# Projection jobs in another order, and the division by ScalarE, in a two-batch attention stage

## Chip, cores, metric

One core of one Trainium2 chip. The time is the device time of one execution of the whole program, in microseconds, the median of 3 runs.

## What is computed

The program is a chain of layers on an input of 2 x 2048 tokens of width 256. The change touches only the attention of layer 1, here with what surrounds it left out:

```python
qkv = x @ W_qkv                                   # x is the normalised input, 16 heads of 64
q, k, v = (to_heads(t) for t in jnp.split(qkv, 3, axis=-1))
q, k = (t * cos + rotate_half(t) * sin for t in (q, k))
dots = jnp.einsum('bhid,bhjd->bhij', q, k) * scale
dots = jnp.where(causal, neg, dots)
attn = jax.nn.softmax(dots, axis=-1)
out = jnp.einsum('bhij,bhjd->bhid', attn, v)
out = jax.nn.relu(out.reshape(b, n, INNER) @ W_o1) @ W_o2     # and a layer norm
```

The other stages (two blockwise FP4 feed-forwards, a selective scan, two mixtures of experts) are the same in both kernels.

## The kernel before

The heads are processed in pairs, 8 pairs a batch, 16 in all (`STREAM`), one after the other as a pipeline. A turn is the work of one pair t, cut into 40 steps (`STEPS`), 20 for each of its two heads. In step v:

- TensorE computes the scores of piece v (`scores`, up to 1024 columns, keys on the partitions, queries in the columns), weighs piece v-2 with the values (`weigh`), peeks at one slot (`peek`: scores with queries on the partitions, only to find each row's maximum) and does a side job if the table `SIDE` has one for this step;
- ScalarE turns piece v into exponents twice, in fp32 (`prob`) and fp16 (`prob_high`), and then does its share of the side job;
- VectorE subtracts the two of piece v-1 (`low_part`), does `take` if piece v-2 ended a chunk, finds the maximum of the peeked slot (`maximum`, one bank, so the next peek waits for it) and does its share of the side job.

Two banks of scores alternate. The weighed sums `o` of one chunk of 512 queries have one bank; its 65th column is the sum of the exponents. A chunk of queries ends with pieces 1, 5, 11 and 19 of each head, so `take` comes at steps 3, 7, 13, 21, 23, 27, 33 and, one turn later, 1. It reads `o`, divides it into `heads`, and only after its `o_taken` may TensorE open the next chunk.

The peeks run ahead (`LEAD` is 24): at step 16 those of the next pair t+1 begin. They need its queries and keys, in chunks of 512 tokens: query chunk 0 and key chunk 0 at step 16, chunks 1 at step 18, query chunk 2 at step 22, query chunk 3 at step 26, key chunk 2 at step 30 and key chunk 3 at step 32. They are made by the 8 `qk` side jobs of pair t+1, numbered i: even i is query chunk i//2, odd i key chunk i//2. For each, TensorE projects (6 matmuls of 512 columns into the one side bank), ScalarE copies the bank to one of two halves of `raw` (after GpSimd has rotated job i-2), SyncE moves it across partitions by four DMAs (`cross`), GpSimd rotates it in five instructions (`rotate`, lines 1880 to 1887), and SyncE stacks it into `q_both` (four DMAs) or `k_twice` and `k_low` (six). SyncE's order is written out: the crossing of i+1, then the stack of i, and after stack 5 the loads of the next weights. At the end `spread_queries` copies the four query chunks once more, into `q_shift`. Other side jobs of a turn are 4 `v` projections, 4 transposes of `heads` (`turn`), 8 output products (`out`) and 2 rows of maxima (`mrow`). A side job waits until the bank of the one before is read.

The first turn (`BEFORE`) only projects pair 0, with its jobs packed into the first steps, and peeks. The last pair has nothing to project.

## Time and profile before

| what | value |
| --- | --- |
| median of 3 runs | 4981.34 us (4978.41 to 4983.54) |
| the profiled execution | 4961.9 us, its span 4960.3 us |
| TensorE, VectorE busy | 3653.6 us (74%), 3715.6 us (75%) |
| ScalarE, GpSimd busy | 2571.2 us (52%), 2373.9 us (48%) |
| granted TensorE clock, mean | 0.869 of full speed |

The profile is of one execution. PE is TensorE (PEld its weight loads), DVE is VectorE, ACT is ScalarE, POOL is GpSimd and SP is SyncE; a q behind a name is that engine's DMA queue. A row of a group names the source line, the engine, the operation, output <- inputs and a count, then the busy time and the mean of one instruction, then how long the engine stood before them and what released it. In a timeline, what stands in brackets at the end is that idle time. Attention fills the stretch from about 2700 to 4475 us.

### The profile page before, as it was taken

How to read it: one execution, taken by the hardware profiler on the slowest of the kernel's cores; microseconds unless marked ns; L12 is line 12 of the kernel's file. 1: busy time of each engine (PE TensorE's matmuls, PEld its weight loads, DVE VectorE, ACT ScalarE, POOL GpSimd, SP SyncE). 2: the span in 40 equal slices, each digit the busy share in tenths (PEclk: the TensorE clock that was granted, in tenths of full speed). 3: DMA queues.
4: the chain of work that ended last, by engine and by line, in shares of the span. 5: the costliest groups of instructions: out<-in, count | busy, mean ns of one | idle time of the engine just before them, and what ended most of it. 6: DMA issues, size and time to landing. Idle time of an engine off the chain costs nothing. (4 is left out here: it accounts for less than half of the span.)

```text
span 4960.3 us, 84705 instructions
## 1 busy us (share of the span) xinstructions
PE 3653.6 (74%) x28907; PEld 2574.3 (52%) x28907; DVE 3715.6 (75%) x4463; ACT 2571.2 (52%) x4134; POOL 2373.9 (48%) x1532
## 2 busy tenths in 40 slices
PE   2997545555555559966945998999989999985495
PEld 1664224444343436655832665666656666664484
DVE  6993589999999989960056998999989899975101
ACT  1222456666666642221312777777767777774131
POOL 0220268888888852202022676665656676600202
PEclk9999877777777779967967999999999999996697
DMA  2000000011000100023632222222222222202254
GB/s 87 0 0 4 7 22 30 30 30 30 30 30 29 31 33 0 0 71 126 190 113 74 54 58 53 59 55 66 55 63 54 54 57 56 54 14 89 81 186 151
DMA packets 236314, 276.23 MB, mean 56 GB/s; under 512 B 63820, under 2 KB 183557, under 8 KB 234561
## 3 DMA queue, kind: packets, MB, share of 16 engines
q1 hardware_dynamic: 223056, 244.85, 18.1%
q0 software_dynamic: 8704, 24.35, 1.4%
q8 instruction: 192, 3.15, 0.3%
q10 hardware_dynamic: 4224, 2.76, 0.3%
q14 instruction: 138, 1.12, 0.1%
HBM read 152.60 MB, written 36.04 MB: 38 GB/s over the span
## 5 line engine op out<-in xcount | busy, mean ns | idle before, releaser
L2255 DVE TENSOR_TENSOR att_b_prob_low<-att_b_prob,att_b_prob_high 128x1024 f16<-128x1024 f32 (+2 forms) x640 | 794.8, 1242 | 63.9 <-ACT att_b_prob_high L2222 61.1
L2220 ACT ACTIVATE att_b_prob<-att_b_score,att_soft 128x1024 f32<-128x1024 f32 (+2 forms) x640 | 633.4, 990 | 218.4 <-PE att_b_score L2133 141.6
L2282 DVE TENSOR_REDUCE att_b_neg_max<-att_b_peek 128x1 f32<-128x1024 f32 (+2 forms) x749 | 666.9, 903 | 47.1 <-PE att_b_peek L2113 31.2
L1030 PE MATMUL mix_scan_hT<-ident,mix_scan_h 128*128 128x128 f32 x1024 | 248.4, 389 | 535.0 <-DVE mix_scan_h L978 500.2
L2222 ACT ACTIVATE att_b_prob_high<-att_b_score,att_soft 128x1024 f16<-128x1024 f32 (+2 forms) x640 | 630.4, 985 | 11.7 <-PE att_b_o L2161 6.6
L1030 PEld LDWEIGHTS mix_scan_hT<-ident,mix_scan_h 128*128 128x128 f32 x1024 | 171.0, 196 | 649.9 <-DVE mix_scan_h L978 442.7
L2157 PE MATMUL att_b_o<-att_b_vh,att_b_prob_high 128*128 128x65 f16 x4352 | 461.8, 195 | 40.1 <-DVE att_b_prob_low L2255 29.3
L2157 PEld LDWEIGHTS att_b_o<-att_b_vh,att_b_prob_high 128*128 128x128 f16 x4352 | 400.8, 98 | 129.7 <-DVE att_b_prob_low L2255 75.9
L2131 PE MATMUL att_b_score<-att_b_q_both,att_b_k_twice 128*128 128x512 f16 (+3 forms) x1280 | 445.6, 348 | 28.7 <-ACT att_b_prob_high L2222 18.5
L2161 PE MATMUL att_b_o<-att_b_vh,att_b_prob_low 128*128 128x65 f16 x4352 | 460.9, 194 | 0.0
L2159 PE MATMUL att_b_o<-att_b_vl,att_b_prob_high 128*128 128x64 f16 x4352 | 460.3, 193 | 0.0
L2133 PE MATMUL att_b_score<-att_b_q_shift,att_b_k_low 65*128 65x512 f16 (+3 forms) x1280 | 441.3, 349 | 0.0
L1422 DVE TENSOR_TENSOR moe_exp_y<-moe_exp_y_ps,moe_b 128x256 f32<-128x256 f32 x64 | 24.2, 420 | 553.3 <-PE moe_exp_y_ps L1370 553.3
L963 DVE RECIPROCAL mix_scan_inv<-mix_scan_inv 128x512 f32<-128x512 f32 x128 | 426.2, 3329 | 13.1 <-POOL mix_scan_inv L840 13.1
L2159 PEld LDWEIGHTS att_b_o<-att_b_vl,att_b_prob_high 128*128 128x128 f16 x4352 | 398.7, 98 | 33.6 <-issue 0.3
L1041 PE MATMUL mix_scan_yT<-mix_scan_hcT,ident 128*128 128x256 f32 x1024 | 414.0, 549 | 0.1
L197 POOL TENSOR_TENSOR ffn_q<-ffn_y,ffn_scale 128x704 f32<-128x704 f32 (+1 forms) x128 | 127.9, 1016 | 597.2 <-DVE ffn_y L191 597.2
L1880 POOL TENSOR_TENSOR att_b_raw<-att_b_raw,att_b_cos 128x512 f32<-128x512 f32 x120 | 182.1, 1517 | 465.4 <-DMA att_b_crossed<-att_b_raw 465.2
L2161 PEld LDWEIGHTS att_b_o<-att_b_vh,att_b_prob_low 128*128 128x128 f16 x4352 | 398.1, 97 | 0.0
L2110 PE MATMUL att_b_peek<-att_b_k_twice,att_b_q_both 128*128 128x512 f16 (+1 forms) x1248 | 345.6, 353 | 42.0 <-DVE att_b_neg_max L2282 33.1
L859 POOL TENSOR_TENSOR mix_scan_dub<-mix_scan_factor,mix_scan_inv 128x1024 f32<-128x1024 f32 x128 | 301.3, 2354 | 38.6 <-POOL mix_scan_inv L855 38.4
L978 DVE TENSOR_TENSOR_SCAN mix_scan_h<-mix_scan_a,mix_scan_state,mix_scan_dub 128x512 f32<-128x512 f32 x256 | 313.1, 1262 | 1.4 <-POOL mix_scan_dub L859 1.4
...
## 6 DMA issues: line engine op xcount, KB each, us to landing
...
mix_scan_b_row<-mix_b_rows SPq DMA_DIRECT2D x128, 256.0 KB, 3.1
att_b_crossed<-att_b_raw SPq DMA_DIRECT2D x512, 64.0 KB, 2.0
att_b_q_both<-att_b_halves SPq DMA_DIRECT2D x240, 64.0 KB, 2.0
att_b_k_twice<-att_b_halves SPq DMA_DIRECT2D x240, 64.0 KB, 2.0
...
```

Source lines behind the costliest of these rows:

```text
L963: dve.reciprocal(one, one).then_inc(inverse_ready, 1)
L1030: last = pe.transpose(hT_ps[:, j * D + m * P:j * D + (m + 1) * P], hs[:, b * W + m * GRP + t * P:b * W + m * GRP + (t + 1) * P], ident[:, :])
L1041: last = pe.matmul(yT_ps[half][:, j * D:(j + 1) * D], ident[:, :], hcT[:, b * W + t * D:b * W + (t + 1) * D], start=(n == 0 and j == 0), s ...
L2131: pe.matmul(out, k_twice[h][:, keys], q_both[h][:, b * SEQ + queries.start:b * SEQ + queries.stop], start=True, stop=False)
L2133: last = pe.matmul(out, k_low[h][0:HEAD + 1, keys], q_shift[h][0:HEAD + 1, queries], start=False, stop=not diagonal)
L2157: pe.matmul(out, prob_high[:, at], v_cols[:, s, 0:HEAD + 1], start=first, stop=False, skip_group_check=True)
L2159: pe.matmul(out_v, prob_high[:, at], vl[:, s * HEAD:(s + 1) * HEAD], start=False, stop=False, skip_group_check=True)
L2161: last = pe.matmul(out, prob_low[:, at], v_cols[:, s, 0:HEAD + 1], start=False, stop=final, skip_group_check=True)
L2220: act.activation(prob[:, at:at + width], score[m % 2][:, 0:width], ACT.Exp, scale=soft[:, 0:1])
L2222: act.activation(prob_high[:, at:at + width], score[m % 2][:, 0:width], ACT.Exp, scale=soft[:, 0:1])\
L2255: dve.tensor_tensor(prob_low[:, at:at + width], prob[:, at:at + width], prob_high[:, at:at + width], ALU.subtract).then_inc(low_ready, 1)
L2282: last = dve.tensor_reduce(neg_max[:, first + col:first + col + 1], peek_bank(kind, s)[:, base:base + nb * P], AX.X, ALU.max, negate=True)
```

## The change

Two independent parts.

First, the list `QK` now says which chunk job i makes, and the steps of jobs 4 to 7 move: query 2 at step 13 (was 12), query 3 as job 5 at step 17 (was job 6 at 18), key 2 as job 6 at step 20 (was job 5 at 15), key 3 at step 24 (was 21). The first three `v` jobs go one step earlier, to 21, 22 and 23. As two query jobs follow each other, the semaphores that count landed stacks are now four, one per kind and per half of the ring, and `rotate`, `spread_queries` and `peek` wait for these.

Second, `take` on VectorE keeps the reciprocal and multiplies the 4 columns of `inv` by a unit, and a new `take` on ScalarE scales the four 64-column parts of `o` into `heads`. It stands behind the exponents of the step and ahead of its side job.

```diff
+QK = [("q", 0), ("k", 0), ("q", 1), ("k", 1), ("q", 2), ("q", 3), ("k", 2), ("k", 3)]
 SIDE = {0: ("qk", 0, 1), 3: ("qk", 1, 1), 4: ("turn", 3, -1), 5: ("out", 6, -1), 6: ("qk", 2, 1), 7: ("out", 7, -1),
-        9: ("qk", 3, 1), 12: ("qk", 4, 1), 15: ("qk", 5, 1), 16: ("mrow", 1, 0), 18: ("qk", 6, 1), 21: ("qk", 7, 1),
-        22: ("v", 0, 1), 23: ("v", 1, 1), 24: ("v", 2, 1), 25: ("turn", 0, 0), 26: ("out", 0, 0), 27: ("out", 1, 0),
-        28: ("v", 3, 1), 29: ("turn", 1, 0), 30: ("out", 2, 0), 31: ("out", 3, 0), 35: ("turn", 2, 0),
+        9: ("qk", 3, 1), 13: ("qk", 4, 1), 16: ("mrow", 1, 0), 17: ("qk", 5, 1), 20: ("qk", 6, 1),
+        21: ("v", 0, 1), 22: ("v", 1, 1), 23: ("v", 2, 1), 24: ("qk", 7, 1), 25: ("turn", 0, 0), 26: ("out", 0, 0),
+        27: ("out", 1, 0), 28: ("v", 3, 1), 29: ("turn", 1, 0), 30: ("out", 2, 0), 31: ("out", 3, 0), 35: ("turn", 2, 0),
...
+        def same_buffer(i):
+            return [u for u in range(QK_JOBS) if QK[u][0] == QK[i][0] and u % 2 == i % 2]
+        def landed(i):
+            return stacked[QK[i][0] + str(i % 2)]
+        def landed_count(p, i):
+            mine = same_buffer(i)
+            return (p * len(mine) + mine.index(i) + 1) * (Q_STACKS if QK[i][0] == "q" else K_STACKS) * 16
...
             if kind != BEFORE or i >= 2:
-                wait_apart(eng, stacked[r], stacked_count(p, i), (tables, 32))
+                wait_for_stack(eng, p, i - 2)
...
-                sp.wait_ge(stacked[0], there)
+                for i in (QK.index(("q", CH - 2)), QK.index(("q", CH - 1))):
+                    there = landed_count(p, i)
+                    sp.wait_ge(landed(i), there if isinstance(p, int) else sp.to_reg(there))
...
                 for v in range(STEPS):
                     if has_piece(kind, v):
                         exponents(t, v)
+                    if v >= 2 and has_piece(kind, v - 2) or v < 2 and has_piece(kind, -1):
+                        take(t, v - 2)
...
+            def take(t, m):
...
+                if h == 0:
+                    wait_unless_first(act, h_turned, turn_count(p - 1, Q + 1))
+                act.wait_ge(inv_ready, chunk_count(p, h, Q) + 1)
+                for i in range(GT):
+                    at = (Q * GT + i) * PAIR + h * HEAD
+                    last = act.activation(heads[:, at:at + HEAD], o_cols[:, i, 0:HEAD], ACT.Identity, scale=inv[:, i:i + 1])
+                last.then_inc(o_taken, 1)
...
-                dve.reciprocal(inv[:, :].unsqueeze(2), o_cols[:, :, HEAD:HEAD + 1]).then_inc(inv_ready, 1)
-                if h == 0:
-                    wait_unless_first(dve, h_turned, turn_count(p - 1, Q + 1))
-                dve.wait_ge(inv_ready, n_chunk + 1)
-                mine = heads[:, Q * GT * PAIR:(Q + 1) * GT * PAIR].rearrange("p (i d) -> p i d", d=PAIR)
-                dve.scalar_tensor_tensor(out=mine[:, :, h * HEAD:(h + 1) * HEAD], in0=o_cols[:, :, 0:HEAD],
-                                         scalar=unit[:, 2:3], in1=inv[:, :].unsqueeze(2).to_broadcast([P, GT, HEAD]),
-                                         op0=ALU.mult, op1=ALU.mult).then_inc(o_taken, 1)
+                dve.reciprocal(inv[:, :].unsqueeze(2), o_cols[:, :, HEAD:HEAD + 1]).then_inc(inv_found, 1)
+                dve.wait_ge(inv_found, n_chunk + 1)
+                dve.tensor_scalar(inv[:, :], inv[:, :], unit[:, 2:3], None, ALU.mult).then_inc(inv_ready, 1)
```

## Rows read from the trace of the kernel before

**Rows 1.** the page: busy time of the engines over the span.

```profile
PE 3653.6 (74%) x28907; PEld 2574.3 (52%) x28907; DVE 3715.6 (75%) x4463; ACT 2571.2 (52%) x4134; POOL 2373.9 (48%) x1532
```

**Rows 2.** stretches: length, busy us per engine (instructions), granted clock, DMA share, GB/s.

```profile
2704.00:4475.00 1771.00, 1629.25 (x20848) 1097.52 (x20846) 1585.37 (x1896) 1316.37 (x1540) 1079.38 (x670) 0.98 0.24 54
3364.65:3473.03 108.38, 101.55 (x1320) 68.74 (x1317) 100.45 (x121) 82.26 (x96) 72.77 (x45) 1.00 0.30 75
```

**Rows 3.** waits in the turn 3364.65 to 3473.03: total us, times, longest.

```profile
ACT att_b_raw L2198 <- POOL att_b_halves L1887: 10.5, 5, 3.2
```

**Rows 4.** timeline of that turn: start, length, engine, operation [idle before <-releaser].

```profile
3399.45 0.59 ACT L2198 COPY att_b_raw<-att_b_side 128x512 f32<-128x512 f32 x1 [2.36 <-POOL att_b_halves L1887]
...
3402.09 2.15 DVE L2255 TENSOR_TENSOR att_b_prob_low<-att_b_prob,att_b_prob_high 128x1024 f16<-128x1024 f32 x1 [1.65 <-ACT att_b_prob_high L2222]
...
3416.57 0.96 DVE L2282 TENSOR_REDUCE att_b_neg_max<-att_b_peek 128x1 f32<-128x768 f32 x1 [0.64 <-PE att_b_peek L2113]
...
3417.03 0.59 ACT L2198 COPY att_b_raw<-att_b_side 128x512 f32<-128x512 f32 x1 [2.90 <-POOL att_b_halves L1887]
...
3418.61 1.21 DVE L2255 TENSOR_TENSOR att_b_prob_low<-att_b_prob,att_b_prob_high 128x384 f16<-128x384 f32 x1 [1.08 <-ACT att_b_prob_high L2222]
...
3424.56 0.59 ACT L2198 COPY att_b_raw<-att_b_side 128x512 f32<-128x512 f32 x1 [3.25 <-POOL att_b_halves L1887]
...
3427.68 0.69 DVE L2299 TENSOR_TENSOR att_b_vl<-att_b_side,att_b_vh 128x512 f16<-128x512 f32 x1 [1.65 <-ACT att_b_vh L2204]
...
3438.65 1.23 DVE L2282 TENSOR_REDUCE att_b_neg_max<-att_b_peek 128x1 f32<-128x1024 f32 x1 [0.97 <-PE att_b_peek L2110]
```

**Rows 5.** same timeline: first, last rotation; last key stack; peek of step 32.

```profile
3371.59 2.16 POOL L1880 TENSOR_TENSOR att_b_raw<-att_b_raw,att_b_cos 128x512 f32<-128x512 f32 x1 [26.95 <-DMA att_b_crossed<-att_b_raw]
...
3443.03 1.16 POOL L1887 TENSOR_TENSOR att_b_halves<-att_b_raw,att_b_halves 128x512 f16<-128x512 f32 x1
...
3447.30 0.60 SPq L1909 DMA_DIRECT2D att_b_k_low<-att_b_halves  x1
...
3455.19 0.38 PE L2110 MATMUL att_b_peek<-att_b_k_twice,att_b_q_both 128*128 128x512 f16 x1 [0.24 <-DVE att_b_neg_max L2282]
```

**Rows 6.** the page, DMA issues: KB each, us from issue to landing.

```profile
att_b_k_twice<-att_b_halves SPq DMA_DIRECT2D x240, 64.0 KB, 2.0
```

**Rows 7.** VectorE's groups in that turn: count | busy us, mean ns | idle.

```profile
L2273 DVE SCALAR_TENSOR_TENSOR att_b_heads<-att_b_o,att_unit,att_b_inv 128x256 f32<-128x256 f32 x8 | 3.9, 484 | 0.6
...
L2268 DVE RECIPROCAL att_b_inv<-att_b_o 128x4 f32<-128x4 f32 x8 | 1.4, 175 | 0.5 <-PE att_b_o L2161 0.5
```

**Rows 8.** timeline around the take at step 33 of that turn.

```profile
3457.89 0.17 DVE L2268 RECIPROCAL att_b_inv<-att_b_o 128x4 f32<-128x4 f32 x1
...
3458.10 0.48 DVE L2273 SCALAR_TENSOR_TENSOR att_b_heads<-att_b_o,att_unit,att_b_inv 128x256 f32<-128x256 f32 x1
3458.50 0.95 DVE L2282 TENSOR_REDUCE att_b_neg_max<-att_b_peek 128x1 f32<-128x768 f32 x1
3458.59 1.11 ACT L2220 ACTIVATE att_b_prob<-att_b_score,att_soft 128x1024 f32<-128x1024 f32 x1
...
3458.73 0.19 PE L2157 MATMUL att_b_o<-att_b_vh,att_b_prob_high 128*128 128x65 f16 x1 [0.41 <-DVE att_b_heads L2273]
...
3459.50 0.55 PE L2110 MATMUL att_b_peek<-att_b_k_twice,att_b_q_both 128*128 128x512 f16 x2
...
3460.50 1.08 DVE L2282 TENSOR_REDUCE att_b_neg_max<-att_b_peek 128x1 f32<-128x896 f32 x1
```

**Rows 9.** ScalarE's groups: exponents in that turn; the scan, whole run.

```profile
L2222 ACT ACTIVATE att_b_prob_high<-att_b_score,att_soft 128x384 f16<-128x384 f32 x8 | 4.7, 586 | 0.6 <-PE att_b_o L2161 0.2
...
L886 ACT ACTIVATE mix_scan_hcT<-mix_scan_hT,mix_CT 128x256 f32<-128x256 f32 x512 | 211.9, 464 | 170.1 <-PE mix_scan_hT L1030 170.1
```

**Rows 10.** ScalarE's timeline: two scan activations; table load ahead of attention.

```profile
1519.43 0.84 ACT L886 ACTIVATE mix_scan_hcT<-mix_scan_hT,mix_CT 128x256 f32<-128x256 f32 x2 [1.53 <-PE mix_scan_hT L1030]
...
2700.03 1.28 ACT L2220 ACT_TABLE_LOAD   x1 [22.00 <-DVE att_b_max_row L2305]
```

54 lines of the change are left out of this document (30 added, 24 removed).

## The prediction, made before the changed kernel was run

> **What bounds the kernel now.** I read the page's busy shares first. VectorE and TensorE are the busiest engines over the whole program [rows 1], but only the stretch that the change touches, the attention of layer 1, counts here. The table of stretches cuts it into turns, one per pair of heads. Both attention batches fill 1771 us. The turn from 3364.65 to 3473.03 us is typical: 108.4 us, VectorE busy 100.5, TensorE 101.6, ScalarE 82.3, GpSimd 72.8, at TensorE's full granted clock [rows 2]. TensorE's busy time counts the drain of pipelined matmuls, so its true load is lower, but VectorE and TensorE are plainly tied: every step hands work from scores to exponents to the low part to the weighing, and peek and maximum share one bank. So a stall lengthens a turn when it stops these two engines together, and ScalarE matters only where it makes them wait.
>
> The waits of that turn say where that happens. ScalarE stood 10.5 us in 5 waits for GpSimd before it could copy a projected chunk; its ring has two places, and GpSimd must have rotated job i-2 first [rows 3]. The timeline shows what each stall did. At step 12 ScalarE waits 2.36 us; the exponents queued behind it come late, and VectorE then stands 1.65. The jobs at steps 18 and 21 hold ScalarE 2.90 and 3.25, and around them VectorE stands 0.64 and 1.08, then 1.65. At step 26 the peek needs the fourth query chunk, whose stack has just landed: VectorE stands another 0.97 [rows 4]. Of these, 0.64 ends on a peek and is the least surely GpSimd's. The sum of these is 1.65 + 0.64 + 1.08 + 1.65 + 0.97 = 5.99 us a turn. Nothing is wrong with GpSimd's total: it is done with the eight rotations at 3444.19 and idle afterwards; the jobs are simply asked for faster (every 3 steps, 8.1 us) than it rotates. From its first step at 3371.59 it rotates six jobs back to back, until 3424.4, 8.8 us each [rows 4, 5].
>
> **The reordering.** Jobs 0 to 3 keep their steps. Query chunk 2 goes from 12 to 13, query chunk 3 from 18 to 17, key chunk 2 from 15 to 20, key chunk 3 from 21 to 24. Count, bytes and matmuls are unchanged. Against the unchanged pace of rotation: job 4 needs the rotation that ended just before 3399.45; ScalarE reaches the copy of step 12 at 3397.1 and gets there one step (2.0 us of exponents) later, so 2.36 falls to about 0.3. Job 5 at 17 finds its place free. Job 6 at 20 needs the end of rotation 4 (3416.9) and comes two steps later than now, which leaves 0 to 1. Job 7 at 24 comes three steps later, which covers 3.25. Query chunk 3 is now job 5, stacked one whole rotation sooner, so the 0.97 goes. I keep 0.7 back for job 6 and for five neighbouring steps (20 to 24) that now all carry side work on TensorE: 5.3 us a turn. Ends: 6.0, and 2.6, the first 1.65 and the 0.97 alone, whose cause the rows name outright.
>
> What is late next is key chunk 3. Its last stack was issued at 3447.30; with 2.0 us to landing [rows 6], it lands at 3449.3, 84.7 us into the turn. The peek of step 32, which needs it, starts at 3455.19, at 90.5 [rows 5]. With 5.3 gained and about 1 given back by then it would start at 86.2, a margin of 1.5 us. On SyncE, job 5 now issues four stacks and job 6 six; the weight loads keep their place behind stack 5, and the crossing of job 7 still queues behind them, so asking for it three steps later costs that rotation little. The copies of the queries into q_shift wait for two counts instead of one, both long met. The prologue's jobs stay packed in steps 0 to 7, ahead of its first peek at 16: nothing.
>
> **The division, VectorE's side.** A take is a reciprocal (0.17) and a scalar_tensor_tensor of 128x256 (0.48) [rows 7]; by starts, 3457.89 to 3458.50, it occupies 0.61 [rows 8]. Afterwards it is the reciprocal, the same 0.21 until its result may be read, and a tensor_scalar of 128x4. No row has it. Bounds: above, what the instruction that it replaces holds VectorE, 0.40 (3458.10 to 3458.50) [rows 8], a gain of nothing; below, the reciprocal of the same 128x4, 0.17 [rows 7], less the 0.08 by which the next instruction starts ahead of an end: 0.1. The size is the reciprocal's, so I take 0.1. VectorE gives up 0.61 - 0.31 = 0.3 us a take, 8 takes a turn: 2.4 us.
>
> **The division, ScalarE's side.** It gets four activations of 128x64 from PSUM with a scale of one column. The selective scan has the same instruction at 256 columns: 464 ns, and two of them in 0.84, so 0.38 from start to start [rows 9, 10]. The exponents take 1.11 at 1024 columns and 0.59 at 384, 0.82 ns a column [rows 8, 9], so 64 columns take 0.16 less than 256: 0.30, and 0.21 apart: 3 x 0.21 + 0.30 = 0.94 us, of which ScalarE is held 0.84; 6.7 us a turn, and its 82.3 becomes 89. Could Identity between Exp ask for a table load? One costs 1.28 and stands once ahead of attention [rows 10]; two a take would be 20 us a turn. But the scan's Identity (line 886, 512 times) runs between the Tanh and Exp of lines 901 and 905, and its group has no load behind it [rows 9]: none is added.
>
> The price is not ScalarE's busy time but the wait it puts into TensorE. The accumulator o has one bank; the weighing that opens the next chunk waits for the take. Now VectorE frees it 0.7 us after its reciprocal starts. Afterwards the take stands in ScalarE's queue behind both exponents of step v, and behind it stand the side copy of that step and the exponents of v+1. At step 33 the exponents end at 3458.59, the four activations would end near 3459.6, and the weighing that opened at 3458.73 (after 0.41 of waiting for VectorE) opens 0.9 later [rows 8]. That delay is not all lost: the next peek would end about 3461.0 instead of 3460.1, and VectorE, which came to it at 3460.50, is 0.3 sooner by its lighter take and waits: the turn loses 0.5. The eight chunk ends (steps 1, 3, 7, 13, 21, 23, 27, 33) differ by the side job that TensorE does in between: where there is a projection (3, 13, 21, 23: about 1.4 us, by the peek's two matmuls in 0.55) TensorE arrives late anyway and the 0.3 may be gained; where there is none or a short one (1, 7, 27, 33) 0.2 to 0.7 is lost. Ends: -0.3 a take (all hidden, VectorE's gain whole) and +0.9 (step 33 everywhere, nothing caught up). I take +0.2, for the majority of the eight lies nearer the lower end: +1.6 a turn. In the last pair there are no peeks in the second half, ScalarE sets the pace and pays 0.84 whole: 5 x 0.84 = +4 once.
>
> **The sum.** 15 turns have both parts (pairs 1 to 15 projected during pairs 0 to 14): 15 x (-5.3 + 1.6) + 4 = -51.5 us. The profiled execution took 4961.9 us (span 4960.3), so 4910 for it; the median of the timed runs is 4981.3, 19 us above, and the same difference gives 4930.
>
> **A rule that speaks against the change.** The take holds VectorE 0.61 us in one instruction of width and would hold ScalarE 0.84 in four [rows 8 to 10]. The Trainium skill (ScalarE: Activation LUTs, Rules for kernel authors) tells to use VectorE, not ScalarE, for a multiplication. By that rule the second part is a loss, which is the second rival below; by the rows it is a loss per take that only matters where TensorE waits.
>
> **Rivals.**
> Both parts pay: the stalls go whole and the takes hide. 15 x (-6.0 - 2.4) = -126 at most, so 4855 to 4905. For it speaks that VectorE is busy for 93% of the turn (100.5 of 108.4); against it, step 33. Chance 0.14.
> ScalarE's take is the new stall (the side of slower): TensorE waits 0.9 at each of the eight chunk ends, 7 us a turn, while the reordering brings its lower end, 2.6: 15 x (7.2 - 2.6) + 4 = +73, up to 5054. With the reordering at 5.3 it decides from a mean of 0.63 us lost per chunk end, and shows from 0.71. For it speaks step 33; against it, the projections that fill the gap at four of eight. Chance 0.13.
> The two cancel within the measurement: 0.55 to 0.71 lost per chunk end, 15 x (-5.3 + 4.4 to 5.7) + 4, 4971 to 4991. Chance 0.12.
> Key chunk 3 becomes the bound: the reordering doesn't do what it says in full, because the peek of step 32 waits for rotation 7 and gives back some 2.5 us a turn: 15 x (-2.8 + 1.6) + 4, 4967. For it: a margin of only 1.5 us. Chance 0.06.
>
> **How the numbers follow.** Forecast 4930, chance 0.55, own range 4905 (stalls gone whole, takes at +0.1: 15 x (-6.0 + 0.8) + 4 = -74) to 4965 (a quarter of the stalls stays, takes at +0.33: 15 x (-4.0 + 2.6) + 4 = -17). The range 4890 to 4988 takes in the cancelling case and the upper part of the first rival. A change under 0.2% (10 us) can't be told from none here. Faster 0.55 + 0.14 + 0.06 = 0.75; same 0.12; slower 0.13.
>
> **What the profile after would show.** Right: in a like turn, ScalarE's waits for GpSimd fall from 10.5 to under 3 us; VectorE's 1.65 waits at steps 14 and 22 are gone; the take's four activations stand about 0.21 apart; turns of 104 to 105.5 us. TensorE's openings wait for ScalarE's heads at steps 1, 7, 27 and 33. Wrong: turns still of 108 with those waits (second rival); peeks of step 32 that wait for a DMA into k_low (the last); projections still waiting for GpSimd at 13 or 20, if rotations stretch beyond 8.8 us.

## The result, and the profile after

The changed kernel takes 5037.77 us in the median of 4 runs (5033.37 to 5043.74), the kernel before 4982.44 (4978.41 to 4987.61): 1.0115 times as long, 95% interval 1.0102 to 1.0128, so 55 us slower. Measured again beside other kernels it was 5034.61 us against 4976.73, a ratio of 1.0124 (1.0108 to 1.0139). The forecast was 4930.

The profiled execution took 5035.53 us. That of before took 4961.9, but 17 of these 73 us lie ahead of the work that the change touches: the selective scan begins at 691.8 us in the one and at 709.0 in the other, which differs from one execution to the next. So the attention of layer 1 is compared by its own length, from the first exponent to the last. The table of stretches of after has the columns of [rows 2]; its two rows are all 16 turns, and the seventh turn, the one whose counterpart stands in [rows 2]:

```profile
2722.10:4519.90 1797.80, 1598.56 (x20745) 1086.50 (x20744) 1602.51 (x1879) 1417.01 (x2030) 1102.77 (x670) 0.98 0.23 52
3397.70:3510.10 112.40, 101.92 (x1322) 69.24 (x1319) 103.26 (x121) 89.38 (x129) 74.00 (x45) 0.98 0.29 72
```

Cut the same way, before is 1746.40 us long, so 51.4 of the 55 us are here. Of these, 8.2 are the last pair's turn alone (84.2 us before, 92.4 after, to the end of the last exponent). The turn went from 108.38 to 112.40 us. ScalarE's busy time rose from 82.3 to 89.4 in it; VectorE's, which was to fall, rose from 100.5 to 103.3.

The waits of that turn, engine and waiting line, what it waited for, total us, times, longest; first ScalarE's, then TensorE's:

```profile
ACT att_b_prob L2254 <- PE att_b_score L2153: 7.4, 9, 1.9
ACT att_b_prob L2254 <- PE att_b_score L2150: 6.4, 11, 1.7
ACT att_b_heads L2243 <- DVE att_b_inv L2304: 3.9, 5, 1.4
...
PE att_b_o L2174 <- ACT att_b_heads L2243: 7.3, 7, 1.7
PE att_b_peek L2127 <- issue: 2.0, 1, 2.0
```

The wait of [rows 3], 10.5 us for GpSimd's rotations, is not among them any more. In its place TensorE waits 7.3 us for ScalarE's heads, at seven chunk ends, and once 2.0 us at a peek. The timeline around the take at step 27 of the turn shows the first of these, with the columns of [rows 8]. Where [rows 8] had 0.21 us from the reciprocal to the division, and the chunk opened at once afterwards, there is now:

```profile
3476.79 0.17 DVE L2302 RECIPROCAL att_b_inv<-att_b_o 128x4 f32<-128x4 f32 x1
3477.00 1.02 DVE L2304 TENSOR_SCALAR att_b_inv<-att_b_inv,att_unit 128x4 f32<-128x4 f32 x1
...
3475.87 2.12 POOL L1895 TENSOR_TENSOR att_b_raw<-att_b_raw,att_b_crossed 128x512 f32<-128x512 f32 x1
...
3478.05 0.93 ACT L2243 ACTIVATE att_b_heads<-att_b_o,att_b_inv 128x64 f32<-128x64 f32 x4 [0.89 <-DVE att_b_inv L2304]
3478.85 1.13 ACT L2254 ACTIVATE att_b_prob<-att_b_score,att_soft 128x1024 f32<-128x1024 f32 x1
...
3479.12 0.19 PE L2174 MATMUL att_b_o<-att_b_vh,att_b_prob_high 128*128 128x65 f16 x1 [1.68 <-ACT att_b_heads L2243]
```

The multiplication of 512 numbers by the unit takes 1.02 us. ScalarE waits 0.89 for it, then needs 0.93, and the weighing opens 0.14 after that, 2.33 us after the reciprocal began; at step 33 of before it was 0.84 [rows 8]. The second wait, at the peek of step 18, follows the stacks of key chunk 1, of which the sixth was issued 0.2 us before TensorE came to the peek:

```profile
3446.40 0.60 SPq L1921 DMA_DIRECT2D att_b_k_low<-att_b_halves  x1
...
3448.56 0.38 PE L2127 MATMUL att_b_peek<-att_b_k_twice,att_b_q_both 128*128 128x512 f16 x1 [1.96 <-issue]
```

The row names "issue", that is, nothing in the profile ends there; in seven other turns the same wait is put down to the DMA into k_low, 16.6 us in seven waits beside 16.9 in seven for "issue". Before, the waits of peeks for k_low were 2.2 us in the whole attention.

### The profile page after: what moved, and what is told of

It is laid out like the page before. It is cut to its first block and busy times, and to the rows that moved or that the text cites. A ratio compares the mean times of both kernels' runs of the same rounds, so it can differ in the third digit from the quotient of the medians.

```text
span 5033.9 us, 85323 instructions
## 1 busy us (share of the span) xinstructions
PE 3660.3 (73%) x28907; PEld 2587.3 (51%) x28907; DVE 3739.0 (74%) x4463; ACT 2679.5 (53%) x4646; POOL 2396.1 (48%) x1532
## 5 line engine op out<-in xcount | busy, mean ns | idle before, releaser
L2289 DVE TENSOR_TENSOR att_b_prob_low<-att_b_prob,att_b_prob_high 128x1024 f16<-128x1024 f32 (+2 forms) x640 | 790.0, 1234 | 34.7 <-ACT att_b_prob_high L2256 29.8
L2174 PE MATMUL att_b_o<-att_b_vh,att_b_prob_high 128*128 128x65 f16 x4352 | 467.0, 195 | 123.6 <-ACT att_b_heads L2243 118.4
L963 DVE RECIPROCAL mix_scan_inv<-mix_scan_inv 128x512 f32<-128x512 f32 x128 | 426.1, 3329 | 12.5 <-POOL mix_scan_inv L840 12.5
L2127 PE MATMUL att_b_peek<-att_b_k_twice,att_b_q_both 128*128 128x512 f16 (+1 forms) x1248 | 344.5, 352 | 51.1 <-issue 16.9
```

What stands on the lines that cost most here:

```text
L963: dve.reciprocal(one, one).then_inc(inverse_ready, 1)
L2174: pe.matmul(out, prob_high[:, at], v_cols[:, s, 0:HEAD + 1], start=first, stop=False, skip_group_check=True)
L2289: dve.tensor_tensor(prob_low[:, at:at + width], prob[:, at:at + width], prob_high[:, at:at + width], ALU.subtract).then_inc(low_ready, 1)
```

## The experiments

**First set: one part at a time.** The change has two parts, and the first question was which of them loses. order_only has the new order of the chunks, with the division as it was; take_only has the old order, with ScalarE's division; unit_folded has the whole change without VectorE's new multiplication. All are timed beside the kernel before (4991.37 us here).

order_only, against the changed kernel:

```diff
-                    if v >= 2 and has_piece(kind, v - 2) or v < 2 and has_piece(kind, -1):
-                        take(t, v - 2)
...
-                dve.wait_ge(inv_found, n_chunk + 1)
-                dve.tensor_scalar(inv[:, :], inv[:, :], unit[:, 2:3], None, ALU.mult).then_inc(inv_ready, 1)
...
+                dve.wait_ge(inv_ready, n_chunk + 1)
...
+                dve.scalar_tensor_tensor(out=mine[:, :, h * HEAD:(h + 1) * HEAD], in0=o_cols[:, :, 0:HEAD],
+                                         scalar=unit[:, 2:3], in1=inv[:, :].unsqueeze(2).to_broadcast([P, GT, HEAD]),
+                                         op0=ALU.mult, op1=ALU.mult).then_inc(o_taken, 1)
```

> The changed kernel, with VectorE's old take (reciprocal and one scalar_tensor_tensor) put back: the reordering alone. Theory A, the take on ScalarE is the whole loss: the reordering alone is faster than before, 4905 to 4965 us, ScalarE's waits for GpSimd gone, but with a new wait of TensorE at the peek of step 18 for key chunk 1 (2 us a turn in the changed kernel's trace). Theory B, the reordering is the loss (five neighbouring side jobs, chunks that land later): slower than before, above 4990 us.

Measured: 4984.38 us (11 runs), 0.9990 of before (0.9981 to 0.9999), between the ranges of the two theories. The new order gains next to nothing, 5 us of the 80 that the prediction gave it. Its trace shows the gain coming and going. The waits of ScalarE for GpSimd fell from 150.5 us in the whole attention to 25.1. By the distance from one step's exponent to the next (medians of seven steady turns) step 12 went from 4.96 to 2.26 us and step 15 from 5.07 to 2.22. But step 17 went from 2.06 to 3.39, step 18 from 3.66 to 6.16, and step 19 from 1.61 to 3.66. Before, TensorE comes to the peek of step 18 at 48.3 us into the turn; now it is there at 46.0, 2.3 us sooner, and the keys are not. The end of the fourth rotation, the last key stack, the peek, and the maximum behind it:

```profile
3426.12 1.44 POOL L1899 TENSOR_TENSOR att_b_halves<-att_b_raw,att_b_halves 128x512 f16<-128x512 f32 x1
...
3430.68 0.60 SPq L1921 DMA_DIRECT2D att_b_k_low<-att_b_halves  x1
...
3432.81 0.59 PE L2127 MATMUL att_b_peek<-att_b_k_twice,att_b_q_both 128*128 128x512 f16 x1 [3.79 <-issue]
...
3433.65 0.82 DVE L2314 TENSOR_REDUCE att_b_neg_max<-att_b_peek 128x1 f32<-128x640 f32 x1 [4.91 <-PE att_b_peek L2130]
```

In the kernel before, in the turn of [rows 2], the same three stand so:

```profile
3405.67 1.71 POOL L1887 TENSOR_TENSOR att_b_halves<-att_b_raw,att_b_halves 128x512 f16<-128x512 f32 x1
...
3410.88 0.60 SPq L1909 DMA_DIRECT2D att_b_k_low<-att_b_halves  x1
...
3413.20 0.43 PE L2110 MATMUL att_b_peek<-att_b_k_twice,att_b_q_both 128*128 128x512 f16 x2 [0.26 <-DVE att_b_neg_max L2282]
```

Key chunk 1 is job 3 in both orders and is asked for at step 9 in both. Before, it lands (2.0 us after its last issue, [rows 6]) at about 3412.9, and the peek starts at 3413.20 with no wait for it: a margin of 0.3 us, which the stalls of steps 12 and 15 had made (in four other turns of before the peek already waited, 2.2 us in all). The new order takes them away, and the peek comes 2.3 us sooner; the keys come 1.5 us later than before (49.7 us into the turn, by the last issue plus 2.0, for 48.2), since the fourth rotation ends later. The two make the wait of 3.79.

Why it ends later can be read from the same rotation. GpSimd's product with the sine and the addition behind it, first in the kernel before, where VectorE stands idle until 3402.09 [rows 4]:

```profile
3400.55 1.26 POOL L1882 TENSOR_TENSOR att_b_crossed<-att_b_crossed,att_b_sin 128x512 f32<-128x512 f32 x1
3401.89 1.26 POOL L1883 TENSOR_TENSOR att_b_raw<-att_b_raw,att_b_crossed 128x512 f32<-128x512 f32 x1
```

and in order_only, where VectorE's subtractions run beside them:

```profile
3418.13 1.87 DVE L2287 TENSOR_TENSOR att_b_prob_low<-att_b_prob,att_b_prob_high 128x1024 f16<-128x1024 f32 x1
3418.88 2.25 POOL L1894 TENSOR_TENSOR att_b_crossed<-att_b_crossed,att_b_sin 128x512 f32<-128x512 f32 x1
3421.21 2.13 POOL L1895 TENSOR_TENSOR att_b_raw<-att_b_raw,att_b_crossed 128x512 f32<-128x512 f32 x1
```

The product is short in all 15 turns of before and long in all 15 of order_only, the addition in 14 of 15 of each. The rotation starts 34.7 us into the turn in both kernels and ends at 42.8 and at 44.6 (medians). So the stall had a second use: while it lasted, GpSimd worked undisturbed, and the prediction's "unchanged pace of rotation" did not hold for the one rotation that mattered.

The wait also costs more than its own length. Within it TensorE's granted clock falls to the lower of its two levels, 1.2 GHz:

```profile
3431.00:3437.80 6.80, 4.99 (x41) 3.52 (x42) 3.99 (x4) 1.16 (x2) 6.34 (x6) 0.50 0.36 80
```

TensorE had stood since 3429.02. Two score matmuls of 512 columns start 0.42 us apart in that stretch (3436.32 and 3436.74), and 0.21 apart at the full clock (3403.61 and 3403.82 in the changed kernel). Over the attention the clock record has 104.1 us at the lower level in order_only, 48.7 in before and 68.3 in the changed kernel. If TensorE set the pace all through the 55 us more of order_only, half of them, 28 us, would be lost; that is an estimate of the most it can cost, and no run measures it alone.

take_only:

```diff
-QK = [("q", 0), ("k", 0), ("q", 1), ("k", 1), ("q", 2), ("q", 3), ("k", 2), ("k", 3)]
+QK = [("q", 0), ("k", 0), ("q", 1), ("k", 1), ("q", 2), ("k", 2), ("q", 3), ("k", 3)]
-        9: ("qk", 3, 1), 13: ("qk", 4, 1), 16: ("mrow", 1, 0), 17: ("qk", 5, 1), 20: ("qk", 6, 1),
+        9: ("qk", 3, 1), 12: ("qk", 4, 1), 15: ("qk", 5, 1), 16: ("mrow", 1, 0), 18: ("qk", 6, 1), 21: ("qk", 7, 1),
...
```

> The changed kernel with the old order and the old steps of the projections: the division by ScalarE alone. Theory A: slower than before by more than the changed kernel is, 5040 to 5110 us: from VectorE's reciprocal to the opening of the next chunk it takes 2.2 us instead of 0.7 at eight chunk ends a turn, and the stalls for GpSimd stay. Theory B: within 10 us of before, 4972 to 4992.

Measured: 5028.85 us, 1.0075 (1.0061 to 1.0089), between the two theories: ScalarE's division alone is a loss of 38 us, and a smaller one than the changed kernel's. TensorE waits 106.1 us for the heads in the whole attention (118.4 in the changed kernel).

unit_folded:

```diff
-                    act.copy(headsT[:, i % 2 * GRP:(i % 2 + 1) * GRP], side_ps[:, :]).then_inc(hT_ready, 1)
+                    act.activation(headsT[:, i % 2 * GRP:(i % 2 + 1) * GRP], side_ps[:, :], ACT.Identity,
+                                   scale=unit[:, 2:3]).then_inc(hT_ready, 1)
-                dve.reciprocal(inv[:, :].unsqueeze(2), o_cols[:, :, HEAD:HEAD + 1]).then_inc(inv_found, 1)
-                dve.wait_ge(inv_found, n_chunk + 1)
-                dve.tensor_scalar(inv[:, :], inv[:, :], unit[:, 2:3], None, ALU.mult).then_inc(inv_ready, 1)
+                dve.reciprocal(inv[:, :].unsqueeze(2), o_cols[:, :, HEAD:HEAD + 1]).then_inc(inv_ready, 1)
```

> The changed kernel without VectorE's multiplication of the 128x4 inverse by the unit; the unit goes into ScalarE's copy of the transposed heads (scale of one column, about 0.1 us more, 4 a turn). It takes 0.74 us on average off VectorE's 8 takes a turn and off the chain that TensorE waits for. Theory A, with that multiplication's wait as the part that was mis-sized: 15 turns x 6 takes x 0.8 us less = about 70 us, 4950 to 5000 us, reciprocal to first activation 0.25 us instead of 1.26. If the four activations are the cost and the multiplication lies beside other work: 5020 to 5040. Theory B: 5030 to 5045.

Measured: 5015.95 us, 1.0046 (1.0033 to 1.0060), between the ranges. Some of the loss goes with the small multiplication, and TensorE's wait for the heads falls to 67.3 us. But the waits for key chunk 1 rise from 33.5 us to 59.2: what the chunk ends give back, step 18 takes again. As long as that wait is there, a difference between two kernels isn't the price of what differs.

**Second set: the wait at step 18.** If the late keys are what holds the new order, peeks that are made later should gain. order_peeks23 makes each 23 steps ahead of its exponents instead of 24, order_peeks22 22 steps. before_peeks23 does the first of these in the old order, as a control. Before was 4988.54 us.

order_peeks23, against order_only:

```diff
-LEAD = STEPS * 3 // 5
+LEAD = STEPS * 3 // 5 - 1
...
-        9: ("qk", 3, 1), 13: ("qk", 4, 1), 16: ("mrow", 1, 0), 17: ("qk", 5, 1), 20: ("qk", 6, 1),
+        9: ("qk", 3, 1), 13: ("qk", 4, 1), 17: ("mrow", 1, 0), 18: ("qk", 5, 1), 20: ("qk", 6, 1),
...
-        36: ("mrow", 0, 1), 37: ("out", 4, 0), 38: ("out", 5, 0)}
+        36: ("out", 4, 0), 37: ("mrow", 0, 1), 38: ("out", 5, 0)}
```

> The new order of the chunks with VectorE's old take (as order_only), and the peeks one step later: each is made 23 steps ahead of the exponents that need it instead of 24 (the maxima's row of head 0 moves from step 36 to 37 behind out 4, that of head 1 and query chunk 3 from 16 and 17 to 17 and 18). Theory (the new order's gain is given back at step 18, whose peek waits 3.8 us a turn for key chunk 1, now the fourth chunk rotated and stacked only after a third query chunk would have been): the peek that needs key chunk 1 comes one step, some 2.7 us, later, its wait falls from 3.8 to about 1.1 us, and 15 turns are 2.6 us shorter each: 38 us below order_only, about 4945 us, turns of 105.5 to 106.5 us. Rival (the wait hides another limit: VectorE and TensorE are bound by their own work, or ScalarE's waits for GpSimd return because all jobs are then asked for faster): the wait shrinks and other idle time takes its place, within 10 us of order_only, 4975 to 4990 us, turns of 108.

Measured: 4963.60 us, 0.9943 (0.9929 to 0.9956). About half way between the two: 21 us below order_only by the medians, 23 by the ratios. The wait is 2.4 us in most turns, not 1.1: TensorE comes to the peek only 1.9 us later in its turn (at 47.9), not a whole step, and the keys come 0.5 later. In all the wait fell from 54.5 to 37.8 us, which is 17 of the 21.

order_peeks22:

```diff
-LEAD = STEPS * 3 // 5
+LEAD = STEPS * 3 // 5 - 2
...
-        9: ("qk", 3, 1), 13: ("qk", 4, 1), 16: ("mrow", 1, 0), 17: ("qk", 5, 1), 20: ("qk", 6, 1),
+        9: ("qk", 3, 1), 13: ("qk", 4, 1), 17: ("qk", 5, 1), 18: ("mrow", 1, 0), 20: ("qk", 6, 1),
...
-        36: ("mrow", 0, 1), 37: ("out", 4, 0), 38: ("out", 5, 0)}
-ROW_AT = {18: (1, 0), 38: (0, 1)}
+        36: ("out", 4, 0), 37: ("out", 5, 0), 38: ("mrow", 0, 1)}
+ROW_AT = {19: (1, 0), 39: (0, 1)}
```

> As order_peeks23, the peeks two steps later than in order_only (22 ahead; both rows of maxima two steps later than there, query chunk 3 stays at 17). Theory: the wait for key chunk 1 is gone, 3.8 us x 15 = 57 us below order_only at most, 4930 to 4950 us, of which something may go back because the maximum of the last peek has two steps less until the first exponents of the next half need it. Rival (another limit takes over): no better than order_peeks23, or slower than it, with a wait of the exponents for the row of maxima at the start of each half.

Measured: 4984.62 us, 0.9993 (0.9984 to 1.0002). The rival's case: the wait for the keys is gone entirely, and the row of maxima, moved two steps later with the peeks, is late instead. At the start of each half the scores wait for its DMA, 61.5 us in 31 waits (step 39 goes from 1.98 to 4.01 us in the median, step 19 to 3.92):

```profile
4164.44 0.52 ACTq L2206 DMA_DIRECT2D att_b_q_shift<-att_b_max_row  x1
...
4166.55 0.39 PE L2148 MATMUL att_b_score<-att_b_q_both,att_b_k_twice 128*128 128x512 f16 x1 [1.79 <-DMA att_b_q_shift<-att_b_max_row]
```

before_peeks23:

```diff
-LEAD = STEPS * 3 // 5
+LEAD = STEPS * 3 // 5 - 1
...
-        9: ("qk", 3, 1), 12: ("qk", 4, 1), 15: ("qk", 5, 1), 16: ("mrow", 1, 0), 18: ("qk", 6, 1), 21: ("qk", 7, 1),
+        9: ("qk", 3, 1), 12: ("qk", 4, 1), 15: ("qk", 5, 1), 17: ("mrow", 1, 0), 18: ("qk", 6, 1), 21: ("qk", 7, 1),
...
-        36: ("mrow", 0, 1), 37: ("out", 4, 0), 38: ("out", 5, 0)}
+        36: ("out", 4, 0), 37: ("mrow", 0, 1), 38: ("out", 5, 0)}
```

> Control: the kernel before with peeks one step later (23 ahead; row of maxima of head 0 from 36 to 37 behind out 4, that of head 1 from 16 to 17). In the old order key chunk 1 is the fourth job behind a stall that delayed the peeks too, and only the peek at step 26 waited for its stacks, 0.3 to 1.2 us a turn. Theory: at most that goes, 0 to 15 us faster than before (4975 to 4991 of 4991). If later peeks were good in themselves (less contention for the shared bank, say), it would gain as much as order_peeks23 does over order_only, some 38 us: then the gain there says nothing of key chunk 1.

Measured: 4988.71 us, 0.9997 (0.9988 to 1.0006). Later peeks bring nothing in the old order, so what they bring in the new one is the wait for the keys.

one_activation, against unit_folded:

```diff
-                for i in range(GT):
-                    at = (Q * GT + i) * PAIR + h * HEAD
-                    last = act.activation(heads[:, at:at + HEAD], o_cols[:, i, 0:HEAD], ACT.Identity, scale=inv[:, i:i + 1])
-                last.then_inc(o_taken, 1)
+                mine = heads[:, Q * GT * PAIR:(Q + 1) * GT * PAIR].rearrange("p (i d) -> p i d", d=PAIR)
+                act.activation(mine[:, :, h * HEAD:(h + 1) * HEAD], o_cols[:, :, 0:HEAD], ACT.Identity,
+                               scale=inv[:, 0:1]).then_inc(o_taken, 1)
```

> As unit_folded (ScalarE's take, the unit folded into the copy of the turned heads), but one activation of 128x256 in place of four of 128x64 per take, with the inverse of the first of the four query blocks for all: it leaves out the division of the other three blocks by their own sums. The chain from the reciprocal to the weighing that opens the next chunk is shorter by 0.93 less about 0.46, 0.47 us. Theory (the chunk ends' chain is the price of ScalarE's take, nearly all of it felt): 8 x 0.3 to 0.47 us a turn, 36 to 56 us below unit_folded's 5016, so 4960 to 4980 (ratio to before 0.993 to 0.998). Rival (the place in ScalarE's queue, behind both exponents and ahead of the side copy and the next exponents, is what costs, not the four's length): less than 15 us below unit_folded, 5000 to 5016.

Measured: 4992.60 us, 1.0009 (1.0000 to 1.0018), 23 us below unit_folded (18 by the ratios): between the two expectations. One activation takes 0.48 us instead of 0.93, and TensorE's waits for the heads fall from 67.3 to 24.9 us. So the length of the four does cost; of the 58 us that 128 takes are shorter in all, 18 to 23 are felt, some 7 of them in the last pair's turn (84.4 us for 91.8).

**Third set: who sets the pace of the keys.** order_fast_rotation and before_fast_rotation shorten GpSimd's rotation in either order, and peeks23_heads goes after what is left of the wait in order_peeks23. Before was 4976.73 us.

peeks23_heads, against order_peeks23 (each head's key stacks are counted on a semaphore of their own; GpSimd waits for both before it writes the buffer again):

```diff
-        stacked = {n: sem("stacked_" + n) for n in ("q0", "q1", "k0", "k1")}
+        stacked = {n: sem("stacked_" + n) for n in ("q0", "q1", "k00", "k01", "k10", "k11")}
...
-                if h == 0 and K_CHUNKS[n + 1] > K_CHUNKS[n]:
+                if K_CHUNKS[n + 1] > K_CHUNKS[n]:
                     job = QK.index(("k", K_CHUNKS[n + 1] - 1))
-                    pe.wait_ge(landed(job), landed_count(p, job))
+                    pe.wait_ge(landed(job, h), landed_count(p, job))
```

> As order_peeks23, but each key chunk's three stacks per head are counted on a semaphore of that head, and a peek waits for those of its own head alone. In order_peeks23 the peek of step 19 still waits 2.4 us in a median turn; the six stacks of key chunk 1 are issued over 3.7 us (3423.05 to 3426.75), head 0's three in the first 1.8. Theory (what is left of the wait is the landing of the last stack): head 0's keys count as there 1.9 us sooner, the wait falls to about 0.5, turns go from 105.4 to about 103.6, 15 x 1.9 = 28 us below order_peeks23, ratio to before 0.9885 to 0.991. Rival (the engines' own work is the next bound at these steps): the wait goes and less than 8 us of time with it, ratio 0.993 to 0.9945.

Measured: 4928.28 us, 0.9903 (0.9888 to 0.9918), as the theory had it. The waits for the keys are 10.0 us in the whole attention. This version is faster than both kernels of the case. All turns and the seventh:

```profile
2719.00:4412.80 1693.80, 1589.54 (x20748) 1083.97 (x20747) 1560.20 (x1880) 1313.39 (x1521) 1118.09 (x670) 0.99 0.24 55
3356.20:3461.20 105.00, 100.17 (x1321) 68.87 (x1318) 99.19 (x121) 82.59 (x97) 74.49 (x45) 1.00 0.31 77
```

A turn is 105.0 us, within the 104 to 105.5 that the prediction named for the whole change, and 3.4 below the turn of [rows 2].

order_fast_rotation, against order_only (before_fast_rotation has the same edit in the kernel before):

```diff
-        ROPE_STEPS = 4
+        ROPE_STEPS = 3
...
-            eng.tensor_tensor(raw[:, ring], raw[:, ring], cos[:, at], ALU.mult).then_inc(rope_step, 1)
-            c.n += 1
-            c.link(eng.tensor_tensor(crossed[:, ring], crossed[:, ring], sin[:, at], ALU.mult))
+            c.link(eng.tensor_tensor(raw[:, ring], raw[:, ring], cos[:, at], ALU.mult))
```

> order_only (new order, VectorE's old take, peeks 24 ahead) with a quicker rotation: it leaves out the multiplication of the crossed halves by the sine, one of GpSimd's five operations of a rotation, 2.25 of 9.3 us. Theory (GpSimd's pace from the first rotation to the fourth sets when key chunk 1 is there, and the new order leaves that untouched): key chunk 1 lands some 6 to 9 us sooner, the 3.8 us wait of step 18 is gone, and turns fall from 108.5 to about 104.5 to 105.5; 45 to 60 us below order_only, 4925 to 4940, ratio to before 0.988 to 0.991. Rival (TensorE's and VectorE's own work around step 18 is the limit and the wait only shows it): within 15 us of order_only, ratio 0.996 to 0.999.

> The kernel before with the same quicker rotation (the sine's multiplication left out). Theory (both orders are held up by the same thing, GpSimd's pace; the old order at steps 12, 15, 18 and 21, the new one at 18): the jobs are asked for every 8.1 us and the rotation now takes some 7.1, so the old order's stalls go as well, and it ends within 10 us of order_fast_rotation, ratio 0.988 to 0.992. Rival (the old order's stalls come from where its jobs stand, not from GpSimd): it keeps most of its 108.5 us a turn, ratio over 0.996.

Measured: 4887.45 us, 0.9809 (0.9795 to 0.9823), and 4897.05 us, 0.9840 (0.9826 to 0.9853). GpSimd's pace holds up both orders: with rotations shorter by one operation ScalarE no longer waits for it in either, no peek waits for keys, and the two orders end 10 us apart. Both gain more than I expected, 90 us against order_only by the ratios where 45 to 60 were foretold, and the waits for keys in order_only were 54.5 in all. So a part is not the waits for keys: GpSimd's busy time in a turn falls from 74.7 to 60.0 us, VectorE's subtractions fall from 780.7 to 740.0 us in all, and TensorE's clock is at its lower level for 32.5 us in place of 104.1. How the gain divides among these, the runs don't tell.

after_again is the changed kernel itself:

> The changed kernel once more, on the same chip and beside the same runs of before as the others, so that the differences to order_only, unit_folded and one_activation can be told with closer intervals: from its first four runs a ratio of 1.0115 (1.0102 to 1.0128). If VectorE's scaling of the inverses costs what the trace says (1.02 us in six of eight takes in place of none), the ratio lies 0.003 to 0.004 above unit_folded's 1.0046, at 1.008 to 1.009; if it is as first measured, 1.010 to 1.013, something beyond that instruction goes with it.

Measured: 1.0124 (1.0108 to 1.0139), the second of the two: 34 to 39 us above unit_folded, where 15 to 20 had been reckoned for the small multiplication. It takes 94.1 us in all 128 takes together. That led to the next run.

**Fourth set: the small multiplication.** In the changed kernel's trace it has two lengths. In the turn above, beside GpSimd's multiplication by the sine, and at step 1, where GpSimd has no work:

```profile
3404.95 2.04 DVE L2289 TENSOR_TENSOR att_b_prob_low<-att_b_prob,att_b_prob_high 128x1024 f16<-128x1024 f32 x1
...
3405.86 2.25 POOL L1894 TENSOR_TENSOR att_b_crossed<-att_b_crossed,att_b_sin 128x512 f32<-128x512 f32 x1
...
3407.11 1.02 DVE L2304 TENSOR_SCALAR att_b_inv<-att_b_inv,att_unit 128x4 f32<-128x4 f32 x1
...
3400.99 0.23 DVE L2304 TENSOR_SCALAR att_b_inv<-att_b_inv,att_unit 128x4 f32<-128x4 f32 x1
```

Of 128 takes, 39 met GpSimd idle and took 0.23 us, all of them; 81 met one of its additions, subtractions or products of two tensors and took 0.85 to 1.15 us, nearly all 1.02; the 8 beside its one-input conversion to f16 took 0.36. In the first rows the multiplication ends at 3408.13 and GpSimd's instruction at 3408.11, and in all 81 the two end within 0.03 us of each other. GpSimd's own instruction is long there as well, 2.23 us in the median (1.27 to 2.32), where the same line takes 1.26 in its quickest. But that is not the multiplication's doing. In all 81 GpSimd's instruction had begun before VectorE's subtraction, which has two inputs in SBUF, was over, and in 75 of them it ended 1.11 to 1.13 us after the subtraction did: as if it had been held until then. The multiplication comes 0.13 us behind the subtraction and so meets nearly all of what is left. In take_only 13 of them come 0.65 us behind it and take 0.51. So the small instruction pays what is left of GpSimd's instruction. The reciprocal ahead of it, which reads PSUM, stays at 0.17 throughout.

The Trainium skill (SBUF — State Buffer, Who interferes with whom) says that VectorE and GpSimd share a pair of ports to SBUF, that a tensor_scalar whose operands allow it may take the pair, and that of two who want it one is fully blocked until the other's instruction ends. The trace agrees: the two end together, 81 times of 81, and the later one comes the less it waits (1.02 and 0.51 us). The page's rule doesn't tell why the multiplication beside the one-input conversion takes only 0.36, though the conversion runs on for 0.86 us after it.

scaled_from_psum, against the changed kernel:

```diff
-                dve.tensor_scalar(inv[:, :], inv[:, :], unit[:, 2:3], None, ALU.mult).then_inc(inv_ready, 1)
+                dve.tensor_scalar(inv[:, :].unsqueeze(2), o_cols[:, :, HEAD:HEAD + 1], unit[:, 2:3], None, ALU.mult).then_inc(inv_ready, 1)
```

> The changed kernel with one operand moved: the tensor_scalar that multiplies by the unit reads the 128x4 sums in PSUM, as the reciprocal before it does, instead of the inverses in SBUF; its output stays in SBUF. Number, order and size of instructions are as in the changed kernel. It leaves out the division: the weighed sums are multiplied by their sums instead. In the changed kernel's trace that instruction takes 0.23 us where GpSimd is idle (39 of 39), 0.36 beside GpSimd's tensor_scalar and 1.02 beside one of its tensor_tensors (the 81 others, but for a few at 0.85 to 0.91). Theory (what lengthens it is GpSimd's use of SBUF, and an operand in PSUM is free of it, as the reciprocal's 175 ns are at every take): 0.2 us at every take, so nearly the time of unit_folded, which lacks the instruction, plus 0.1 to 0.2 a take: 8 x 15 x 0.6 x 0.3 to 0.5, some 20 to 35 us below the changed kernel, ratio to before 1.005 to 1.008. Rival (its output in SBUF, or the wait for the reciprocal's result, makes it long): a mean of 0.7 us or more as before, ratio 1.011 to 1.0125.

Measured: 4992.15 us, 0.9996 (0.9986 to 1.0006), further down than either expected. The two groups, of the changed kernel and of this one (the whole attention):

```profile
L2304 DVE TENSOR_SCALAR att_b_inv<-att_b_inv,att_unit 128x4 f32<-128x4 f32 x128 | 94.1, 735 | 4.5
```

```profile
L2304 DVE TENSOR_SCALAR att_b_inv<-att_b_o,att_unit 128x4 f32<-128x4 f32 x128 | 28.4, 222 | 4.5
```

0.22 us at every take: it was the operand in SBUF. The like place in this kernel has the same subtraction and the same long GpSimd instruction, and the multiplication is done 0.77 us before it:

```profile
3426.06 2.25 DVE L2289 TENSOR_TENSOR att_b_prob_low<-att_b_prob,att_b_prob_high 128x1024 f16<-128x1024 f32 x1 [0.16 <-ACT att_b_prob_high L2256]
...
3427.18 2.25 POOL L1894 TENSOR_TENSOR att_b_crossed<-att_b_crossed,att_b_sin 128x512 f32<-128x512 f32 x1
...
3428.44 0.22 DVE L2304 TENSOR_SCALAR att_b_inv<-att_b_o,att_unit 128x4 f32<-128x4 f32 x1
```

GpSimd's two-input instructions beside the multiplication last 2.24 us in the median here, as long as in the changed kernel, so it was the subtraction and not the multiplication that lengthened them. From the first to the last exponent the program is 44 us shorter (59 to 64 by the ratios). The chains at the chunk ends, from a chunk's last weighing to the next one's first, are 1.9 us a turn shorter (23.2 for 25.1, medians of eight summed), which is 29 us. The waits for keys are another 14: the fourth rotation ends 42.7 us into the turn instead of 45.2 (median), and ten of the 15 turns have no wait for key chunk 1 at all.

**Fifth set: the same three forms of the division where that wait is away.** unit_folded and scaled_from_psum contradict each other if taken as prices: with no multiplication at all 1.0046, with a short one 0.9996. So each form was put on peeks23_heads. Before was 4975.88 us; the edits are those shown above.

> peeks23_heads (new order, peeks 23 ahead, keys counted per head) with the changed kernel's take: ScalarE's four activations and VectorE's tensor_scalar that reads the inverses in SBUF. Theory (the long scaling, 1.02 us in six takes of eight, and the four activations stand between the last weighing of a chunk and the first of the next, and with the wait of step 18 gone nothing absorbs them): the steps other than 18 and 19 cost 6.5 us a turn more than with VectorE's take (median turns of the changed kernel against order_only), so 15 x 6.5 = 97 us above peeks23_heads, ratio 1.008 to 1.010. Rival (what the changed kernel lost against order_only, 3.5 us a turn, is the take's whole price and the wait absorbed nothing): about 53 us above, ratio 1.000 to 1.002.

> As best_after_take, with the scaling instruction reading its operand in PSUM (the weighed sums are multiplied by their sums instead of divided: the division is left out). Theory (the operand in SBUF is most of the loss): the chunk ends' chains are 2.0 us a turn shorter than with it, 30 us or more below best_after_take, and still above peeks23_heads, by 2 to 4 us a turn: ratio 0.996 to 1.003. Rival (in the earlier pair the 43 us between the two came from the phase of the rotations at step 18, not from the operand): within 15 us of best_after_take.

> As best_after_take, without a scaling instruction (the unit is folded into ScalarE's copy of the turned heads, as in unit_folded). Theory (moving the division to ScalarE costs by its own four activations and their place in the queue, 2 us a turn in the steps other than 18 and 19): 25 to 35 us above peeks23_heads, ratio 0.995 to 0.998, and not above best_take_psum, whose chain is 1.5 us a turn longer. Rival (ScalarE's take is free once nothing else is late; VectorE's time is what it buys): at or below peeks23_heads, ratio up to 0.991.

Measured: 5013.39 us, 1.0076 (1.0062 to 1.0090); 4962.23 us, 0.9972 (0.9961 to 0.9983); 4967.52 us, 0.9983 (0.9974 to 0.9992). The second lies in its theory's range, the first just under (1.008), the third just above (0.998); that it would not lie above the second is not borne out, though the two are only 0.0011 apart, within their intervals. A like turn of each, in this order:

```profile
3386.20:3498.10 111.90, 100.12 (x1319) 68.50 (x1315) 105.09 (x121) 89.03 (x128) 74.14 (x45) 1.00 0.29 72
```

```profile
3366.90:3474.50 107.60, 100.25 (x1321) 68.45 (x1318) 100.43 (x121) 89.01 (x128) 73.90 (x45) 1.00 0.30 75
```

```profile
3371.80:3479.20 107.40, 100.36 (x1321) 68.52 (x1318) 97.48 (x113) 88.94 (x128) 75.75 (x45) 1.00 0.30 75
```

ScalarE is busy alike in the three, and 6.4 us more than in peeks23_heads; the turn is 2.4 to 2.6 longer than there for that, and 4.3 more where the multiplication reads SBUF. By the ratios, moving the division to ScalarE costs 0.0069 to 0.0080 of the time, 34 to 40 us, and the operand in SBUF another 0.0104, 52 us. The ratio of peeks23_heads, measured beside other runs of before, has an interval of 0.0015 to either side, 7 us.

All in one table, with sums over the whole attention, in us:

| kernel | ratio to before | first to last exponent | ScalarE waits for GpSimd | peeks wait for keys | TensorE waits for the heads |
| --- | --- | --- | --- | --- | --- |
| before | 1 | 1746.4 | 150.5 | 2.2 | 10.0 |
| changed | 1.0115 | 1797.8 | 2.8 | 33.5 | 118.4 |
| order_only | 0.9990 | 1743.1 | 25.1 | 54.5 | 13.3 |
| take_only | 1.0075 | 1788.3 | 60.8 | 3.5 | 106.1 |
| unit_folded | 1.0046 | 1779.9 | 12.5 | 59.2 | 67.3 |
| scaled_from_psum | 0.9996 | 1753.7 | 6.2 | 19.6 | 85.1 |
| order_peeks23 | 0.9943 | 1723.0 | 24.4 | 37.8 | 12.2 |
| peeks23_heads | 0.9903 | 1693.8 | 54.1 | 10.0 | 12.3 |

## Why the prediction was wrong

It missed by 108 us (5038 against 4930). By the parts: the order was to bring 15 x 5.3 = 80 us and brought 5 (order_only); the division was to cost 15 x 1.6 + 4 = 28 and cost 62 to 67 on top of that order (1.0115 and 1.0124 less 0.9990). 75 and some 36 make the 108 within what the ratios leave open.

**The reordering: the step that failed is "what is late next".** The stalls were right: the waits for GpSimd went from 10.5 us to none in the turn, jobs 4 to 7 found their places free, and so was the reason, since a shorter rotation frees both orders. But I looked for the next late chunk only among those that the change moves. Key chunk 3, which I named with its margin of 1.5 us, was never late in these runs. Key chunk 1 was, a job that the change leaves at its step, because it was asked for no later, needed 2.3 us sooner, and had 0.3 us of margin in the trace that I had before me. The rows were there: the issue of its last stack at 3410.88 and its peek at 3413.20. With it failed a premise, "against the unchanged pace of rotation": the fourth rotation took 9.9 us instead of 8.1, for VectorE no longer stood still beside it. The waits for keys, 54.5 us in all, and at most some 28 for the lower clock behind them cover the 75 us that the order did not bring; how the 75 divide was not measured. The rival that names key chunk 3 had the mechanism, a peek that waits for its keys and gives the gain back, and its chance of 0.06 was far too small for the mechanism as such; its place was wrong.

**The sum of 5.99 us was also counted as if idle time removed were turn removed.** With the wait for the keys nearly gone (peeks23_heads) the order is worth 3.4 us in the like turn and 48 us over all, 3.2 us a turn. That is nearer to my lower end, 2.6, than to the 5.3 that I took. That version moves the peeks as well, and is no measurement of the reordering alone.

**The division, VectorE's side: a term mis-sized, from the wrong neighbour.** The scaling was set at 0.1 us with 0.4 as its upper bound, the hold of the instruction that it replaces. Both neighbours, the reciprocal and the scalar_tensor_tensor, read PSUM; the scaling reads SBUF beside a GpSimd that is busy for 73 us of 108 in the turn. It took 0.74 us in the mean and 1.02 in most: outside both bounds. A pair of bounds taken from neighbours holds only if they share what makes the price, and here they did not. The wait for GpSimd, which had no term in the sum, is what was missing. It costs 52 us, and with it the part that was to gain VectorE 2.4 us a turn made it busier by 4.6 (103.2 us in the like turn, 98.6 in order_only). Had it been the 0.22 that it is from PSUM, the estimate of 0.1 would have been near enough.

**ScalarE's side: mechanism and sizes right, the balance low.** Four activations take 0.93 us (0.94 foretold), the turn's busy time is 89.4 (89), no table load was added, and the weighing opens 0.14 us behind the last of them. (The working has 0.94 from 3 x 0.21 + 0.30, which is 0.93, and the 0.21 is 0.22 by its own rows; neither matters.) With the scaling away the move costs 34 to 40 us over 128 takes, 0.27 to 0.31 each, where I took 0.2 between ends of -0.3 and 0.9. The projections cover less than assumed: TensorE waits for the heads at 116 of the 128 takes in the changed kernel, not at half. The last pair was set at +4 us once and cost 8.2; 7.6 of these are there in unit_folded, which has the four activations and no multiplication, and 0.2 in one_activation.

**The rivals.** The second one, ScalarE's take as the new stall, comes nearest: the sign, and its range up to 5054. By the profile it holds as far as TensorE waits for the heads at nearly every chunk end; but a little more than half of that loss is VectorE's scaling, which the rival didn't name, and the order brought 0.3 us a turn, not its lower end of 2.6. The Trainium skill's rule that a multiplication belongs on VectorE (ScalarE: Activation LUTs, Rules for kernel authors) came out on its side as well: all three forms of ScalarE's division are slower than VectorE's one instruction of 0.48 us, by 34 to 86 us on the best order.

**The two parts together** lose more than the sum of each alone: 0.9990 and 1.0075 would make 1.0065, and 1.0115 to 1.0124 was measured, some 25 us more. The steps show where: at step 23 the take costs 1.4 us more than order_only's in the new order and 0.6 more than before's in the old; at step 27 it is 1.4 against 0.65. At step 23 the multiplication is most of it: 0.37 us in take_only, 1.02 in the changed kernel (medians), by what GpSimd does at that moment. In all 128 takes it is 66.7 us for 94.1, 27 less. That the old stalls covered a part of the takes as well is not shown.

**Left open.** Between before and order_only the rows show why the fourth rotation ends at 42.8 or at 44.6 us into the turn. Among the forms of ScalarE's division, where it ends between 42.5 (best_take_psum) and 46.1 (best_take_folded), it was not followed. Each of its instructions has two lengths, as 1.26 and 2.25 us, by what VectorE does beside it, and a small shift of the two against each other moves the keys by 2 to 3 us.
